# Decoder layer with ternary FFN on one core: the ternary units made and checked before the gate/up stage and kept in DRAM

## What is computed

```python
x = layernorm(x + attn(x, wq, wk, wv, wo))        # 32 query heads, 8 key/value heads of 128,
                                                  # causal, each row sees the last 128 keys
x = layernorm(x + fake_quant(x) @ fake_quant(ctx)) # 8-bit grid, ctx is 2 x 1024 x 1024
x = layernorm(x + ffn(x))

def ffn(x):                                       # w_gate, w_up: 2752 x 1024, w_down: 1024 x 2752
    gate, up = (x / 128) @ w_gate.T, (x / 128) @ w_up.T
    inter_q = trunc(clip(silu(gate) * up * 128, -128, 127))
    return trunc(clip((inter_q @ w_down.T) * 128, -128, 127))
```

## Time and profile before

| | us |
|---|---|
| median of 3 runs | 1550.74 (1546.24 to 1550.97) |
| the profiled execution | 1546.86 |
| its span, first to last instruction | 1545.1 |
| TensorE busy | 1484.5 (96%) |
| VectorE, ScalarE, GpSimd busy | 963.9 (62%), 785.7 (51%), 851.3 (55%) |
| chain that ended last | TensorE 85%, VectorE 6%, ScalarE 4% |
| mean granted TensorE clock | 0.986 of full |
| 16 DMA engines, queue 1 | 217.48 MB, 40.0% of their time |

### The profile page before, as it was taken

The page is one execution under the profiler, slowest core; times in us unless marked ns, Lnnn a source line. Parts: engine busy times, 40 slices in busy tenths (PEclk is TensorE's granted clock), DMA queues, the critical chain, the costliest instruction groups (busy, mean ns, idle before and its releaser), DMA issues.

```text
span 1545.1 us, 23314 instructions
## 1 busy us (share of the span) xinstructions
PE 1484.5 (96%) x7516; PEld 1215.4 (79%) x7533; DVE 963.9 (62%) x1505; ACT 785.7 (51%) x1572; POOL 851.3 (55%) x753
## 2 busy tenths in 40 slices
PE   7899999999999999999999999998799999999796
PEld 6788888888888788888888888875478888887443
DVE  7644444444346566666666666668667777767597
ACT  5433333333344455454545454625766676666564
POOL 4577777776455454545545455435677667666000
PEclk9999999999999999999999999999899999999998
DMA  6377777775324533424252333402023232332111
GB/s 218 142 275 275 273 278 277 278 274 209 130 102 154 212 114 125 149 75 149 68 173 93 131 119 123 162 3 81 16 69 121 82 122 98 106 121 83 55 41 70
DMA packets 83477, 218.14 MB, mean 141 GB/s; under 512 B 8416, under 2 KB 8800, under 8 KB 83424
## 3 DMA queue, kind: packets, MB, share of 16 engines
q1 hardware_dynamic: 83424, 217.48, 40.0%
HBM read 153.49 MB, written 63.96 MB: 141 GB/s over the span
## 4 chain that ended last, share of the span: by engine, by line
PE 85%; DVE 6%; ACT 4%; issue 2%; DMA 1%; POOL 1%; SPq 1%; ACTq 0%; DVEq 0%; POOLq 0%
PE ps L813 9%; PE ps L815 9%; PE ps L814 9%; PE ps L1044 8%; PE ps L1045 8%; PE ps L881 7%; PE ps L882 7%; PE ps L883 7%; PE ps L1072 5%; PE ps L863 2%; PE ps L833 2%; PE ps L864 2%; PE ps L834 2%; PE ps L832 2%; PE ps L845 2%
## 5 line engine op out<-in xcount | busy, mean ns | idle before, releaser
L1044 PE MATMUL ps<-xt_h,w_h 128*128 128x512 f32 x704 | 276.8, 393 | 5.9 <-ACT w_h L1412 5.9
L1045 PE MATMUL ps<-xt_l,w_h 128*128 128x512 f32 x704 | 275.7, 392 | 0.0
L813 PE MATMUL ps<-xo_h,wb_h 128*128 128x512 f32 x644 | 252.1, 391 | 7.0 <-issue 6.1
L814 PE MATMUL ps<-xo_l,wb_h 128*128 128x512 f32 x644 | 251.5, 391 | 0.0
L815 PE MATMUL ps<-xo_h,wb_l 128*128 128x512 f32 x644 | 251.5, 391 | 0.0
L1719 POOL TENSOR_TENSOR pm_l<-pt_l,upto 128x512 fp32r<-128x512 f32 x64 | 83.1, 1299 | 250.7 <-DVE pt_l L1974 250.7
L881 PE MATMUL ps<-wo_h,o_h 128*128 128x512 f32 x512 | 206.5, 403 | 1.2 <-DMA wo_l<-wo_low 0.9
L882 PE MATMUL ps<-wo_l,o_h 128*128 128x512 f32 x512 | 199.8, 390 | 0.0
L883 PE MATMUL ps<-wo_h,o_l 128*128 128x512 f32 x512 | 199.6, 390 | 0.0
L1044 PEld LDWEIGHTS ps<-xt_h,w_h 128*128 128x128 f32 x704 | 133.3, 189 | 35.1 <-ACT w_h L1412 3.9
L1688 POOL TENSOR_TENSOR wb_l<-wf_l,wb_h 128x512 fp32r<-128x512 f32 x69 | 90.0, 1304 | 128.2 <-ACT wb_h L1184 64.3
(11 more groups left out here) (185 smaller groups left out, 3349.8 us busy)
## 6 DMA issues: line engine op xcount, KB each, us to landing
raw<-w_att SPq DMA_DIRECT2D x47, 512.0 KB, 5.4
wp_raw<-w_att SPq DMA_DIRECT2D x32, 512.0 KB, 5.8
wo_high<-wp_h SPq DMA_DIRECT2D x32, 512.0 KB, 2.8
wo_low<-wp_l SPq DMA_DIRECT2D x32, 512.0 KB, 4.1
q_rows<-c SPq DMA_DIRECT2D x64, 256.0 KB, 2.5
q_raw<-q_rows SPq DMA_DIRECT2D x64, 256.0 KB, 2.6
wo_h<-wo_high SPq DMA_DIRECT2D x16, 1024.0 KB, 5.2
wo_l<-wo_low SPq DMA_DIRECT2D x16, 1024.0 KB, 7.4
```

Source lines behind the costliest of these rows:

```text
L813: pe.matmul(prod_ps[i], wh, chunk(xo_h[i], c), start=(i in OPENS and c == 0), stop=False, skip_group_check=True)
L814: pe.matmul(prod_ps[i], wh, chunk(xo_l[i], c), start=False, stop=False, skip_group_check=True)
L1044: pe.matmul(dst, w, xt_h[:, c, rows], start=(c == 0), stop=False)
L1045: last = pe.matmul(dst, w, xt_l[:, c, rows], start=False, stop=(c == DC - 1))
```

## The change

The units of all 66 weight tiles of 128 x 1024 (44 of gate and up, 22 of down) are made and compared before the norms, and written to two new DRAM tensors, `u_gu` in float32 and `u_dn` in bfloat16. 18 tiles are handled in the quads 18 to 21 of the projections (8 gate/up, 10 down; at the products of `EARLY_STEPS`), and one tile in each slot of the attention groups 1 to 6 (six gate/up and two down in a group). A tile takes: SP loads the raw tile (512 KB), ACT makes the unit (`make_tile`), DVE compares it (`check_tile`) and adds the count (`add_misfits`), SP stores the unit (512 KB, down 256 KB). There are two buffers of each kind. In a slot SP does this last, ACT last, DVE ahead of the second addition into `resid`. `find_sizes` moves ahead of quad 18; ACT waits there for the stores of the output weights, and ahead of the first attention slot for all early checks and stores.

The branch moves ahead of the gate/up stage. In the gate/up stage SP loads `w_h` and `d_unit` straight from the new tensors; the makes, POOL's and DVE's checks, ACT's counts and the trip of `resid[:, 0:2]` to DRAM are gone. The diff, cut:

```diff
+UNITS_FROM = HQ // 2 + HEADS_FROM
+EARLY_STEPS = (1, 2, 4, 5), (1, 2, 4, 5), (0, 1, 2, 4, 5), (0, 1, 2, 4, 5)
+EARLY_GU, EARLY_D = 8, 10
...
+        u_gu = nc.dram_tensor("u_gu", (FC, 2, P, DM), F32).ap()
+        u_dn = nc.dram_tensor("u_dn", (FC + 2, P, DM), BF16).ap()
...
@@ SP
+            def load_tile(g, s):
+
+                n = s if g is None else g * UNITS + (s - UNITS)
+                wait(sp, fu_checked, n - 1)
+                sp.dma_start(f_raw[place_of(s)][:, :], tile_of(g, s, w_gu, w_down)).then_inc(fr_loaded[s % 2], 16)
+
+            def keep_tile(g, s):
+                n = s if g is None else g * UNITS + (s - UNITS)
+                sp.wait_ge(fu_made, n + 1)
+                unit = f_down[place_of(s)][:, :] if is_down(s) else plain(f_unit[place_of(s)][:, :])
+                sp.dma_start(tile_of(g, s, u_gu, u_dn, 2), unit).then_inc(fu_kept[s % 2], 16)
+
+            def tiles_slot(g, j, first, last):
+
+                if first:
+                    return
+                if not last:
+                    if j > 0:
+                        keep_tile(g, EARLY + j - 1)
+                    load_tile(g, EARLY + j)
+                    if j == UNITS - 1:
+                        keep_tile(g, EARLY + j)
...
                     else:
                         load_context(g * 2 + (j // 2 - 2), j // 2)
+                tiles_slot(g, j, first, last)
...
+                for k, i in enumerate(PRODUCTS):
+                    s = early_tile(n, k)
+                    if s is not None and s >= 2:
+                        keep_tile(None, s - 2)
+                        load_tile(None, s)
                     keep(n, i)
...
+            def load_units(c, k, before):
+                if before is not None:
+                    sp.wait_ge(u_done, before)
+                for i in range(2):
+                    sp.dma_start(plain(w_h[:, 2 * k + i, :]), u_gu[c, i]).then_inc(u_loaded[k], 16)
...
+                load_units(2, 0, 3)
+                load_units(3, 1, 4)
+                with sp.Fori(1, PAIRS - 1) as pair:
+                    for k in range(2):
+                        load_units(pair * 2 + (2 + k), k, pair * 4 + (2 + 2 * k))
+                        load_down(pair * 2 + (k - 2))
@@ PE
+                    pe.wait_ge(path_chosen, 1)
...
+            pe.wait_ge(misfit_row, 1)
+            pe.wait_ge(y_added, OUT_BLOCKS - 12)
+            pe.matmul(bank(0)[:, 0:1], ones_bf[:, :], misfit[:, :], start=True, stop=True).then_inc(misfit_sum, 1)
...
-                pe.wait_ge(u_made, 2 if first else pair * U_PAIR + (3 * i + 1))
+                pe.wait_ge(u_loaded[i], pair * 32 + 32)
@@ ACT
+            def make_tile(g, s):
+
+                e = s % 2
+                n = s // 2 if g is None else g * (UNITS // 2) + (s // 2 - UNITS // 2)
+                act.wait_ge(fr_loaded[e], n * 16 + 16)
+                wait(act, fu_kept[e], n * 16)
+                act.activation(unit_at(s)[:, :], f_raw[place_of(s)][:, :], ACT.Copy, scale=param(INV_G + size_of(s))).then_inc(fu_made, 1)
...
                     scale_context(k, odd, loads)
+                if not first and not last:
+                    make_tile(g, EARLY + j)
...
+            act.wait_ge(sizes_ready, 1)
+            for e in range(2):
+                act.wait_ge(wp_kept[e], 16 * HQ)
...
+            act.wait_ge(fu_checked, EARLY)
+            for e in range(2):
+                act.wait_ge(fu_kept[e], 16 * EARLY // 2)
             for j in range(UNITS):
                 slot_of(0, j, True, False)
...
+                for m in range(4):
+                    unit_silu(pair, m)
+                    unit_size(pair, m)
+                    if m > 0:
+                        unit_store(pair, m - 1, first or last)
+                    elif not first:
+                        unit_store(pair - 1, 3, False)
+                    if last and m == 2:
+                        stage(0)
@@ DVE
+            def check_tile(g, s):
+
+                n = s if g is None else g * UNITS + (s - UNITS)
+                dve.wait_ge(fu_made, n + 1)
...
+                if s >= 1:
+                    add_misfits(n - 1, s - 1)
+                dve.scalar_tensor_tensor(out=raw, in0=unit, scalar=param(SIZE_G + size_of(s)), in1=raw, op0=ALU.mult,
+                                         op1=ALU.not_equal, accum_out=misfits[:, 1 + s % 2:2 + s % 2]).then_inc(fu_checked, 1)
...
                     probs_low(g, j - 1)
+                if not first and not last and j > 0:
+                    check_tile(g, EARLY + j - 1)
                 if not events:
                     add_slot(g, j, 1, last)
                 if j % GROUP == 0:
                     value_low(g, j // GROUP)
+                if not first and not last and j == UNITS - 1:
+                    check_tile(g, EARLY + j)
```

More of the change, by code:

```diff
@@ L157, in build @@
         at_t = xo_at[PS3]
+        fr_at = (at_k + 26624, at_k + 30720, at_t, at_t + 4096)
+        fu_at = (at_k + 22528, at_k + 34816, at_t + 8192, at_t + 12288)
+        f_raw = [place(f"f_raw{e}", [P, DM], F32, fr_at[e]) for e in range(4)]
+        f_unit = [place(f"f_unit{e}", [P, DM], F32R, fu_at[e]) for e in range(4)]
+        f_down = [place(f"f_down{e}", [P, DM], BF16, fu_at[e]) for e in range(4)]
         x_scaled = place("x_scaled", [P, 2, DM], F32, at_t)
@@ L684, in _ @@
                             load_head((head + 2) // GROUP, (head + 2) % GROUP + e, e, None)
+            for s in range(EARLY - 2, EARLY):
+                keep_tile(None, s)
             for j in range(UNITS):
@@ L1139, in _ @@
             with pe.Else():
-                pe.wait_ge(u_product, 2 * FC)
+                pe.wait_ge(y_added, OUT_BLOCKS)
+                for i in range(TILES + 2, TILES + 5):
+                    slot(i)
+                pe.wait_ge(xq_ready, TILES)
+                pe.wait_ge(shift_ready, TILES)
+                pe.wait_ge(cross_added, TILES)
+                pe.wait_ge(x2_low, TILES)
                 for m in range(4):
@@ L1379, in scale_rows @@
                 act.wait_ge(ln_done[0], t + 1)
+                if t == 0:
+                    act.wait_ge(misfit_row, 1)
+                    for e in range(2):
+                        act.wait_ge(fu_kept[e], 16 * U_TILES // 2)
                 wait(act, x_quant, t - 1)
@@ L1503, in down_counted @@
-                def down_counted(n, tiles):
-                    act.wait_ge(ud_checked, tiles)
-                    count(n, d_raw[:, :])
-                unit_silu(pair, 0)
-                count_gate_up(first_chunk(pair, first), pair * 4, 0)
-                unit_size(pair, 0)
-                down_made(0)
-                if not first:
-                    unit_store(pair - 1, 3, False)
-                unit_silu(pair, 1)
-                if not first and not last:
-                    next_made(0)
@@ L1532, in unit_pair @@
-                unit_silu(pair, 3)
-                if not last:
-                    next_made(1)
-                unit_size(pair, 3)
-                unit_store(pair, 2, first or last)
-                if not last:
-                    down_counted(second_down(pair, False), pair * 2 + 2)
+                for m in range(4):
+                    unit_silu(pair, m)
[6 more added lines that the diff above has]
+                        stage(0)
@@ L2057, in _ @@
                         behind(r * 2 + odd, i, r * 2 + (odd + 1), r + odd, 1 - odd, True)
-            for n in range(HQ // 2 + HEADS_FROM, QUADS - 4):
-                for i in PRODUCTS:
+            find_sizes()
+            for n in range(UNITS_FROM, QUADS - 2):
+                for k, i in enumerate(PRODUCTS):
                     behind(n, i, n + 1, (n + 1) // 2, (n + 1) % 2, True)
-            for n in range(QUADS - 4, QUADS - 2):
-                for i in PRODUCTS:
-                    behind(n, i, n + 1, (n + 1) // 2, (n + 1) % 2, True)
+                    s = early_tile(n, k)
+                    if s is not None and s > 0:
+                        check_tile(None, s - 1)
+            check_tile(None, EARLY - 1)
             dve.wait_ge(consts, CONSTS)
@@ L2231, in with_sign, with unit_product @@
                                                 in1=sizes.bitcast(U32), op0=ALU.bitwise_and, op1=ALU.bitwise_or)
-            def unit_product(pair, m, last):
+            def unit_product(pair, m):
                 n = pair * 4 + m
-                check = m in (1, 2 if last else 3)
                 dve.wait_ge(u_silu, n + 1)
@@ L2258, in unit_truncate, with unit_pair @@
                 with_sign(sizes, sizes, u_val[:, m % 2, :]).then_inc(u_signed, 1)
-            def unit_pair(pair, first, last):
-                for m in range(3 if last else 4):
-                    unit_product(pair, m, last)
+            def unit_pair(pair, first):
+                for m in range(4):
+                    unit_product(pair, m)
                     if m > 0:
```

313 lines of the change are left out of this document (114 added, 199 removed).

## The result

| | us |
|---|---|
| changed kernel, median of 4 runs | 1715.88 (1712.28 to 1719.78) |
| kernel before, median of 4 runs beside it | 1548.51 (1546.24 to 1550.97) |
| ratio | 1.1087, 95% interval [1.1072, 1.1103] |
| forecast | 1674 (1590 to 1740) |

The change makes the kernel 167 us slower. The forecast had the sign and the main mechanism; it is 42 us short.

The account below looks back on a forecast made before the run. TensorE, busy for 96% of the span, was taken to bound the kernel. 1546.9 us profiled + 136.8 (attention) - 2 + 6 (projections) + 1 - 18.1 (gate/up and down) = 1670.6; with 3.9 for the median 1674 us, range 1590 to 1740.

Parts of the forecast that it names:

- Gate/up and down: Stage after attention: both waits on `w_h` go, the `lhs` wait shrinks, slow clock behind gaps goes: -18.1 us (-14 to -20).
- the branch's +1: Ahead of gate/up: reading the path and branching on TensorE stands in the open, +1 us (0 to 2).
- the `lhs` wait: TensorE's 7.39 us wait on `lhs`, released by ScalarE: 1 us left (0 to 3), 6.4 us won.
- the closed loop: Attention groups 1 to 6: late raw tile delays copy, query and next tile; +22.8 us a group, +136.8 for six.
- TensorE's lead: Attention: TensorE had 2.1 us in hand from the mask's end to `values`, taken as -2 us.
- the store's term: Attention slots: of 4.85 us for store and load ahead of the make, a full store takes 1.8.
- the signs that I named: Changed trace: raw-tile waits 2 to 3 us, 6 to 8 in slots 4 and 6; group some 93, TensorE idle over 20.
- The projections: Quads 18 to 21: 18 early tiles mostly fit in, two new full stops cost ScalarE; +6 us (0 to 12).
- In time: Rival, attention: tiles land by the make in every slot, group stays 70.6 us, total 1537; chance 0.11.
- Only the `wo` slots bind: Rival, attention: plain slots keep 8.7 us, only slots 4 and 6 lengthen; +94 us, total 1632; chance 0.12.
- a tile overtakes `wo`: Rival, attention slots 4 and 6: the tile does not queue behind `wo`; +55 us for six groups, total 1593; chance 0.07.
- The clock did fall: Rival, attention: TensorE's clock falls for good among small gaps, +30 to +60 us, total past 1700; beyond 1740 chance 0.06.

Follow-up runs that it names:

- two of the experiments: Changed kernel with all three edits, 1549.20 us; and the same with the next quad's raw weights loaded behind the third product, 1545.04 us.
- the last kernel: Kernel with all three edits, plus the next quad's raw weights loaded behind the third product in quads 18 to 21: 1545.04 us.
- all three edits: Changed kernel with raw tile issued at each attention slot's head, early tiles checked, stored and loaded one product behind the make, and full stops relaxed: 1549.20 us.
- the best order found: Kernel with all three edits, plus raw weights of the next quad loaded behind the third product: 1545.04 us, 0.9983 of before.

## Why the prediction was right or wrong

**Gate/up and down: right.** -19.0 for -17.1 (with the branch's +1), and -20.3 and -21.5 in two of the experiments. Both waits on `w_h` are gone; the `lhs` wait left 0.48 us where I left 1, the last one 0.20 where I left 0.63.

**Attention, the closed loop: right in mechanism and nearly in size.** The periods from `copy_current` to the next in the changed kernel, read from the timeline of ScalarE at 954.53 to 1050.84 us, beside the forecast:

| slot | 0 | 1 | 2 | 3 | 4 | 5 | 6 | 7 | sum |
|---|---|---|---|---|---|---|---|---|---|
| forecast | 10.45 | 10.25 | 11.35 | 9.35 | 17.25 | 10.25 | 15.95 | 8.55 | 93.4 |
| measured | 11.71 | 10.19 | 10.75 | 9.94 | 17.64 | 10.58 | 16.12 | 9.38 | 96.3 |

Issuing the tile earlier took the loop away (-141 us), a second store ahead of it lengthened it, and the same store where no tile stands behind it cost a tenth of that. Three things were off. The mean group is 96.0, not 93.4: in the group shown, slot 0 takes 1.3 us more, as its context is issued 4.3 us behind the copy and not 3.7 and the tile behind it comes later than the 1.5 us I gave it, and the slots 3 and 7 take 0.6 and 0.8 more. I subtracted 2 us of TensorE's lead; in a loop that TensorE doesn't close there is no lead to subtract, and six groups gained all of 152.5. And the store's term was too dear: I charged a full one 1.8 us and a half-size one 0.8; a second one costs 1.3 to 1.7 and 0.5. Moving it behind the load is worth less still (4.5 us a group for 11.5), since it delays the tile from behind in three slots and GpSimd's masks take back 2.3 us. That the sum for store and load came out near enough is in part luck: the load must then have taken more than I had left for it. Of the signs that I named, the waits came out longer (1.9 to 4.5 us for 2 to 3, 8.35 and 9.51 for 6 to 8), and TensorE is idle for 16.6 us of the group and not for over 20: its slower clock fills a part of the loop.

**The projections: wrong, by 31 us, and the step is this one:** "ScalarE has the makes for the `head_high` it had. It waits for its tile there, as SP issues it about one product (2.7 us) ahead, but the blocks it makes are for the next quad." ScalarE's blocks are, but its `first_sum` and VectorE's result sums belong to the quad in hand, and they are queued behind the make and the check. I had named `first_sum` as standing behind the two full stops, and those were worth 1.8 us; behind each of the 18 tiles I did not ask. The experiments give the parts of the 37.2 us, each give or take the spread of 2.5: tiles loaded and checked too late 23.3, stops 1.2 on top of that, raw weights ahead of the tiles 6.2, and 6.4 that no run took away. In the trace of the last kernel 4.9 of these 6.4 us are waits of TensorE, 3.4 for `first_sum` and 1.5 for a result sum of VectorE, so they are of the same kind. VectorE's checks are a candidate for a part (2.6 us with all three edits, not tried beside the last one); the rest stays open. "At lower volume per quad" was false: by the sizes that I had myself, two heads are 3 MB in a quad and the tiles 3.75 to 4. But the volume was no answer either: the same share of the DMA engines hides in one order and not in another. The term's own range, 0 to 12, was missed by 25 us; the total lies in the stated range because attention's part of it was wide.

**The rivals.** "In time" (1537) is what the tile first gives to attention, but not in the order of the change. "Only the `wo` slots bind" falls by the periods of the plain slots. That a tile overtakes `wo` falls by the slots 4 and 6 (17.64 and 16.12). The Trainium skill, page "DMA: Bandwidth & Descriptors", section "Queues, rings and completion order", says that each ring is worked in order; these two slots agree. The clock did fall, to 0.93 over the six groups, but it was not the cause: `copy_current` never waits for TensorE there, and with the tile first the clock is 1.00 again. The time was not past 1740.

**The sum.** 45.9 us short in the span: projections 31.2, attention 17.7, the other two stages -3.0. The median stood 1.2 above its profiled span, where I had added 5.7. Three readings in the prediction were off without bearing on this: TensorE's lead in the earlier trace rows is 2.2 us and not 2.1, the store and the load end 2.7 us beyond `q_raw`'s landing by my own terms and not 3.0, and the upper end that I worked out, 1747, lies outside the range that I gave.

## What to carry to other kernels

Work that is put into a slot with idle engines costs what its wait costs, not what it takes: find where in the issuing queue its load comes, and whether that issue depends on the slot before. If it does, the way to that issue, then landing and use, is the slot's shortest time, and moving one line in SP's order can be worth 141 us with every instruction kept. For every wait that is added to an in-order engine, list what is queued behind it on that engine, at every place where it is added and not only at the conspicuous ones. When a loop is shortened, look for the next chain that holds it. And before a stage is unloaded into others, ask what the others will pay: here a gain of 21.5 us was met by 16.6 at the best order found.

## What the runs showed of the hardware

**A check on VectorE holds GpSimd up.** `pm_l` (64 products of two SBUF tiles) took 1299 ns before. In the changed kernel the 64 have a mean of 1971 ns, from the same group of the page:

```profile
L1713 POOL TENSOR_TENSOR pm_l<-pt_l,upto 128x512 fp32r<-128x512 f32 x64 | 126.1, 1971 | 252.4 <-DVE pt_l L1945 252.4
```

One of them, and VectorE's check that began 0.09 us earlier, in the timeline of all engines:

```profile
970.91 1.28 DVE L1994 SCALAR_TENSOR_TENSOR f_raw<-f_unit,prm,f_raw 128x1024 f32<-128x1024 f32 x1
...
971.00 2.33 POOL L1713 TENSOR_TENSOR pm_l<-pt_l,upto 128x512 fp32r<-128x512 f32 x1 [3.93 <-DVE pt_l L1945]
```

2.33 is the 1.30 of before and 1.03 more, and 1.19 us of the check were left. The Trainium skill, page "SBUF — State Buffer", section "SBUF: two separate sides", says that an operation of VectorE with two SBUF inputs and one of GpSimd that reads SBUF exclude each other, and that the one which starts first has the ports for the whole instruction; these rows agree. It can go the other way: the check at 411.44 above takes 2.39 us for 1.28, beside this product of GpSimd, which takes its usual time:

```profile
411.46 1.28 POOL L1682 TENSOR_TENSOR wb_l<-wf_l,wb_h 128x512 fp32r<-128x512 f32 x1
```

The starts lie 0.02 us apart, too near to tell from the rows which came first. The forecast had the check at 0. It cost GpSimd 1 us in a slot; with the tile first TensorE waited for the mask for 1.7 us in all six groups, and with the store behind this 1 us stands in the chain that held the query.

**Neighbouring transfers share the engines.** A 512 KB store issued 0.5 us behind a 512 KB load delayed it as much as one issued 0.5 us ahead in the slots 1, 2 and 5 (5.4 for 5.3 us from issue to make, 6.4 for 6.0, 5.4 for 5.2), and by 0.5 to 1.1 us less in 3, 4 and 6 and, half-size, in 7. In 1, 2 and 5 a value or context transfer stands between the query and the tile; whether that sets them apart no run shows. A second full store ahead lengthened the same way by 0.8 to 1.0 us in every slot that has one.
